# Adding products by a 1 MB transfer or on GpSimd in turns, and four more transposes on VectorE, in an embedding tower on one core

## What is computed

```python
e = jnp.stack([tbl_f[ids[:, f]] for f in range(40)], axis=1)     # 512 x 40 x 64, fp32
i_idx, j_idx = triu_indices(40, k=1)                             # 780 pairs
viW = einsum('bpd,pde->bpe', e[:, i_idx], W)                     # W: 780 x 64 x 64
z = einsum('bpe,bpe->bp', viW, e[:, j_idx])                      # 512 x 780
h = concatenate([z, dense_ctx], axis=1)                          # 512 x 796
h = maximum(h @ W_top1 + b_top1, 0)                              # 796 x 512
h = maximum(h @ W_top2 + b_top2, 0)                              # 512 x 256
y = h @ W_top3                                                   # 256 x 1
```

## Time and profile before

| what | us |
|---|---|
| median of three runs | 319.62 |
| span of the profiled execution | 361.1 |
| TensorE busy | 324.8 |
| VectorE busy | 255.2 |
| GpSimd busy | 206.5 |
| ScalarE busy | 106.8 |
| mean granted TensorE clock | 0.957 of full speed |

### The profile page before, as it was taken

How to read it: one execution, slowest core, us unless ns; L and a number is a source line. 1 busy time by engine, 2 the same in 40 slices (tenths; PEclk the granted TensorE clock), 3 DMA queues, 4 the chain that set the end, 5 groups by cost and what they waited for, 6 DMA issues and landing times.

```text
span 361.1 us, 4423 instructions
## 1 busy us (share of the span) xinstructions
PE 324.8 (90%) x1700; PEld 115.7 (32%) x1700; DVE 255.2 (71%) x249; ACT 106.8 (30%) x266; POOL 206.5 (57%) x178
## 2 busy tenths in 40 slices
PE   7999739699888949949959999989999999999997
PEld 2444213133222313312312333333333333333455
DVE  5996535586676856945847899999999999990000
ACT  0216000060505551350767653025049000001032
POOL 3887737354735625634654538989987677770000
PEclk9999988899989969987998999999999999999999
DMA  7941212112212272302211346867798766650000
GB/s 170 337 154 51 60 32 66 43 47 73 57 42 53 78 257 92 79 21 52 73 51 42 81 86 147 176 145 158 151 193 172 170 136 118 117 109 9 15 0 0
DMA packets 17772, 35.34 MB, mean 98 GB/s; under 512 B 3924, under 2 KB 4952, under 8 KB 17624
## 3 DMA queue, kind: packets, MB, share of 16 engines
q0 software_dynamic: 7408, 16.26, 23.4%
q1 hardware_dynamic: 7848, 13.96, 12.9%
q10 hardware_dynamic: 2496, 4.84, 3.9%
HBM read 22.86 MB, written 0.00 MB: 63 GB/s over the span
## 4 chain that ended last, share of the span: by engine, by line
PE 59%; DVE 19%; issue 8%; POOL 6%; another core or an unknown queue 6%; DMA 1%; ACT 0%; DVEq 0%; POOLq 0%
PE y_ps L664 33%; PE z_ps L687 15%; DVE prod L558 14%; PE y_ps L697 4%; POOL prod L378 3%; POOL gathered L349 2%; DVE prod L484 2%; PE t_ps L697 2%; PE y_ps L743 1%; PE t_ps L571 1%; POOL prod L374 1%; DMA lane_rows_sb<-lane_rows 1%; DVE zT L494 1%; DVE x_quad L490 1%
## 5 line engine op out<-in xcount | busy, mean ns | idle before, releaser
L664 PE MATMUL y_ps<-x,w 64*128 64x512 f32 x780 | 190.0, 619 | 29.6 <-DVE prod L558 21.9
L349 POOL DMA_INDIRECT gathered<-in_tbl,ids_sb x128 | 131.2, 1025 | 94.6 <-DVE prod L558 55.9
L558 DVE TENSOR_TENSOR prod<-y_ps,x 128x1024 f32<-128x1024 f32 x89 | 103.8, 1216 | 54.8 <-PE y_ps L664 27.5
L664 PEld LDWEIGHTS y_ps<-x,w 64*128 64x128 f32 x780 | 70.6, 189 | 146.6 <-issue 104.0
L558 DVE TENSOR_TENSOR prod<-y_ps,x_quad 128x1024 f32<-128x1024 f32 x96 | 110.6, 1215 | 3.8 <-PE y_ps L664 1.9
L687 PE MATMUL z_ps<-prod,select 128*32 128x512 f32 x596 | 81.7, 652 | 1.2 <-POOL prod L378 1.2
L417 ACT COPY x<-x_fold 32x128 f32<-32x128 f32 x176 | 52.0, 295 | 84.2 <-DVE x_fold L527 70.6
L378 POOL TENSOR_TENSOR prod<-prod 128x1024 f32<-128x1024 f32 x23 | 55.3, 2406 | 0.8
L374 POOL DMA_DIRECT2D prod<-prod x23 | 21.6, 939 | 22.4 <-DVE prod L558 16.3
L687 PEld LDWEIGHTS z_ps<-prod,select 128*32 128x32 f32 x596 | 15.3, 114 | 59.4 <-issue 39.5
L440 ACT COPY x_mix<-x 64x512 f32<-64x512 f32 x40 | 24.7, 616 | 0.7
(11 more groups left out here) (47 smaller groups left out, 84.8 us busy)
## 6 DMA issues: line engine op xcount, KB each, us to landing
w<-w_rows SPq DMA_DIRECT2D x48, 256.0 KB
prod<-prod POOLq DMA_DIRECT2D x23, 512.0 KB, 4.6
gathered<-in_tbl,ids_sb POOLq DMA_INDIRECT x128
w<-w_rows ACTq DMA_DIRECT2D x1, 1792.0 KB
prod<-in_tbl ACTq DMA_DIRECT2D x6, 256.0 KB
prod<-hot_ids SPq DMA_DIRECT2D x4, 256.0 KB, 3.9
prod<-in_tbl ACTq DMA_DIRECT2D x4, 128.0 KB, 3.3
w<-w_rows ACTq DMA_DIRECT2D x1, 512.0 KB
```

What stands on the lines that cost most here:

```text
L349: nc.gpsimd.indirect_dma_start(gathered[:, slot, c, s * DIM:(s + 1) * DIM], None, tables[f][:, :], bass.IndirectOffsetOnAxis(ap=ids_sb[:, ...
L558: nc.vector.tensor_tensor(prod[:, d % PROD_SLOTS, :, :], y_ps[:, d % DUO_SLOTS, :, :], factor, ALU.mult).then_inc(prod_ready, 1)
L664: last = nc.tensor.matmul(y_ps[:, d % DUO_SLOTS, half, :], w[rows, r % W_SLOTS, d % ROUND, :], x[rows, units[half], :], start=True, stop=True)
```

## The change

Units 12 and 13 become quads too (`PAIRED` 14 to 12), so that quads start at round 17 instead of 23 or 24. In rounds of `ADDED_BY_DMA` one accumulating DMA adds both duos (1 MB), in rounds of `ADDED_BY_POOL` one GpSimd instruction does (128x2048). 27 rounds are added: 17, 19, 21 and 24 to 47. Sums go three rounds behind (`LAG`). `FOLDED` starts at unit 5, `INSIDE` is 7, and 24 gathers are free at the start. With these `transposed_at` is 6 for units 5 and 6, 9 for unit 7, and 17, 25, 33, 41 for units 8 to 11; then 52, 60, 68, 80, 88, 100, 120, 144.

```diff
-LAG = 2
+LAG = 3
-PAIRED = 14
+PAIRED = 12
-FOLDED = range(9, 20)
-INSIDE = 3
-GATHERED_FIRST = 16
-ROUND_GATHERS = [4] * 24
-LATE_GATHERS = [1, 1, 2, 1, 1, 3, 1, 2, 1, 2, 1]
-UNADDED = [29]
+FOLDED = range(5, 20)
+INSIDE = 7
+GATHERED_FIRST = 24
+ROUND_GATHERS = [4] * 17 + [3] * 7
+LATE_GATHERS = [2, 1, 2, 1, 2, 1, 2, 1, 1, 1, 1]
+ADDED_BY_DMA = [17, 19, 21, 24, 26, 28, 30, 32, 34, 36, 38, 40, 42, 44, 46]
+ADDED_BY_POOL = [25, 27, 29, 31, 33, 35, 37, 39, 41, 43, 45, 47]
...
             for r in range(len(plan.rounds)):
-                if r in plan.added:
-                    done = gather_up_to(ROUND * r + ROUND - 1)
-                    nth = plan.added.index(r)
-                    low = ROUND * r % PROD_SLOTS
-                    pool.wait_ge(prod_ready, ROUND * r + 3)
+                done = gather_up_to(ROUND * r + ROUND)
+                low = ROUND * r % PROD_SLOTS
+                lows, highs = prod[:, low:low + 2, :, :], prod[:, low + 2:low + 4, :, :]
+                if r in ADDED_BY_DMA:
+                    nth = ADDED_BY_DMA.index(r)
+                    pool.wait_ge(prod_ready, ROUND * r + 4)
                     if nth >= PROD_ROUNDS:
                         pool.wait_ge(accumulated[nth % PROD_ROUNDS], 16 * (nth // PROD_ROUNDS))
-                    nc.gpsimd.dma_start(prod[:, low, :, :], prod[:, low + 2, :, :],
-                                        accum_op=ALU.add).then_inc(accumulated[nth % PROD_ROUNDS], 16)
-                    done = gather_up_to(ROUND * r + ROUND)
+                    nc.gpsimd.dma_start(lows, highs, accum_op=ALU.add).then_inc(accumulated[nth % PROD_ROUNDS], 16)
+                elif r in ADDED_BY_POOL:
                     pool.wait_ge(prod_ready, ROUND * r + 4)
-                    nc.gpsimd.tensor_tensor(prod[:, low + 1, :, :], prod[:, low + 1, :, :], prod[:, low + 3, :, :],
-                                            ALU.add).then_inc(added, 1)
-                else:
-                    done = gather_up_to(ROUND * r + ROUND)
+                    nc.gpsimd.tensor_tensor(lows, lows, highs, ALU.add).then_inc(added, 1)
...
-                if r in plan.added:
-                    nth = plan.added.index(r)
-                    pe.wait_ge(added, nth + 1)
+                duos = range(ROUND * r, ROUND * r + 2)
+                if r in ADDED_BY_DMA:
+                    nth = ADDED_BY_DMA.index(r)
                     pe.wait_ge(accumulated[nth % PROD_ROUNDS], 16 * (nth // PROD_ROUNDS + 1))
-                    duos = range(ROUND * r, ROUND * r + 2)
+                elif r in ADDED_BY_POOL:
+                    pe.wait_ge(added, ADDED_BY_POOL.index(r) + 1)
...
-            sum_round(len(plan.rounds) - LAG)
+            for r in range(len(plan.rounds) - LAG, len(plan.rounds) - 1):
+                sum_round(r)
```

More of the change, by code:

```diff
@@ L107, in __init__ @@
         self.gather_times()
-        self.added = [r for r in range(self.quad_start[0], len(self.rounds)) if self.is_quad(r) and r not in UNADDED]
+        assert all(self.is_quad(r) for r in ADDED_BY_DMA + ADDED_BY_POOL)
     def gather_times(self):
@@ L118, in gather_times @@
             after += [max(ROUND * r - 1, 1)] * count
-        assert len(ROUND_GATHERS) == self.quad_start[0] + 1 and len(after) == parts * (UNITS - HOT_UNITS)
+        assert len(after) == parts * (UNITS - HOT_UNITS)
         self.gather_after = after
```

## The result

The changed kernel takes 339.95 us (median of four runs, 339.28 to 340.61); the kernel before took 319.56 us beside it. The ratio is 1.0641, with a 95% interval of 1.0619 to 1.0662: slower by 20 us. Forecast were 337.0 us and a range of 326 to 343.

The account below looks back on a forecast made before the run. TensorE's own order was taken as the bound nearly throughout, VectorE close behind in added rounds. On 319.6 us, -3.4 - 1.2 - 2.4 + 0.6 + 16.6 + 4.3 + 2.9 = +17.4 gave 337.0 us, range 326 to 343.

Parts of the forecast that it names:

- The start: VectorE's queue waits for gathers of units 6 and 7 at their early transposes, and TensorE runs dry: +16.6 us.
- ScalarE's order at block 0: Unit 11's copies and mixtures stand ahead of block 0's copy in round 10, so sum 8 waits: +4.3 us.
- The duos stay 195: Regrouping leaves the count of duos at 195; only added rounds change, from 23 to 27.
- Four transposes off TensorE (-2.4): Units 5 to 8 leave TensorE, 4 x 0.59 us, for VectorE transposes and 16 ScalarE copies each: -2.4 us.
- Additions (-1.2): TensorE's present wait on GpSimd's addition goes: -1.2 us.
- Four more added rounds (-3.4): Added rounds go from 23 to 27, each saving TensorE 0.85 us in its sum: -3.4 us.
- Unit 18's transpose in an added round (+0.6): Unit 18 (duo 120, round 30) now meets an added round, where VectorE lacks time for its transpose: +0.6 us.
- neither wait is there, 313.2: Rival: gathers land before product 6 and ScalarE reaches its copy in time, 313.2 us; chance 0.05.
- The clock: TensorE's clock halves after the new waits, 1.7 us after sum 8 and 1.2 at the start: +2.9 us.
- Quicker gathers in the runs: Rival: gathers start 0.94 us apart in the runs, not 1.25; 332.4 us, or some 329; chance 0.05.
- ScalarE's wait alone, 319.2: Rival: the start is not exposed and only ScalarE's wait stays, 319.2 us; chance 0.05.
- The late transfer: Rival: the 1 MB transfer lands after its 12.0 us window; one us more costs 12, 349 us; chance 0.07.

Follow-up runs that it names:

- the second profile of before: The kernel before, unchanged, profiled once more: span 319.3 us in an execution of 321.1 us.
- the two mended kernels: Changed kernel with transposes of units 5 to 13 re-placed and two mixture-buffer sets, 321.06 us; same but units 5 to 8 transposed by TensorE, 320.84 us.
- the 16 gathers: Against the mended kernel with TensorE's transposes, only the first field of units 10 to 13 gathered, 16 gathers fewer: 315.85 us, ratio 0.9878.

## Why the prediction was right, and where it was not

**The start: right.** Foreseen were unit 6's landing at 45.8 (44.3), unit 7's at 55.8 (54.2), and the end of sum 1 at 69.4 (69.0). Against the second profile of before, whose TensorE stood there at 53.6, the start costs 15.4. That has the half clock in it, so it stands against 16.6 + 1.2 = 17.8: 2.4 less than foreseen. Of this 0.8 is the point of before (53.6, not 52.8), and some 1.5 is that the 24th gather started at 41.81, not 43.27. It varies between executions, from 41.81 to 45.46 in the profiles, so that part is luck. The landing was taken as 2.5 between bounds of 1.0 and 3.8 and is 2.5. The text's choice of starts 1.25 apart rather than spans of 0.94 was right too: by the spans the forecast would have been 332.4.

**ScalarE's order at block 0: right, the size a little small.** Foreseen were 4.3 of wait and 1.7 of half clock; the profile has 5.0 and 1.75. The rest of the 7.2 us between the sums is 0.4: unit 11's transpose itself waited 0.8 for its gathers. The runs without it gained 4.1; in the profile the difference lies in the start of that execution, and how it spreads over the runs stays open.

**Round 23: missed.** The step that failed is the regrouping, costed by the count of duos alone ("The duos stay 195"). A duo that was moved also moves the release of the buffer that it reads. It costs 4.2 us in the profile (sum 21 comes 8.80 after sum 20 instead of 4.63), 3.1 in the runs. The forecast's error of 3.0 is what is left of larger ones: 4.2 here and 1.2 at block 0 too little, 2.4 at the start too much. The mechanisms at the start and at block 0 are as foreseen; that 337.0 came within 1% is in part because these errors cancel.

**The terms of TensorE's work: true in the changed kernel, worth less once the waits are gone.** TensorE is busy 311.4 us, against 310.5 in the second profile of before. Of that 6.7 is half clock: four stretches of 3.1 to 3.5 us at 0.50, busy throughout. Without it TensorE's work is 5.8 less, which is 2.4 + 3.4. In the time, too, the terms add up: 15.4 + 7.2 + 4.2 - 3.4 - 1.2 - 2.4 + 0.6 = 20.4, as measured. They are not worth that by themselves. Four transposes off TensorE (-2.4): nothing, as the two mended kernels show, 321.06 and 320.84; ScalarE's 16 copies a unit come in between. Additions (-1.2): 0.3 to 0.6. Four more added rounds (-3.4): the regrouping that brings them needs unit 13 in round 17 instead of 20, and the new order asks for units 12 to 14 eight duos sooner; GpSimd's pace takes the gain back. Only with the transposes placed by that pace is 1.4 us left of all terms. Unit 18's transpose in an added round (+0.6) costs 0.4. The step that failed is the one behind the rival "neither wait is there, 313.2": it held that TensorE is the bound nearly throughout once the two waits are gone. It is not, over the first 14 units. The first profile hid it: from 36 to 162 us it has 71 gathers where the second has 97. Gathers are released by products, which came late there, so GpSimd's pauses looked like slack.

**The clock: right in kind.** 2.9 were foreseen. The profile has half-clock stretches after each of the four waits, as in the earlier trace rows; those after block 0 and round 23 cost about 1.7 us each (3.60 for 1.85 in the one seen above), and the latter was not foreseen. Those of the start partly fall into VectorE's pace, and no run parts the two. "Rounds of 4.63 from 27 on" came out, but for 5.00 twice, at the transposes of units 18 and 19, and no sum waits for a transfer for more than 0.8 us.

**The rivals.** Quicker gathers in the runs: no; from the 13th on the starts are 1.25 apart in every kernel's profile wherever nothing holds them back, and the profiled execution took 339.51 us, like the others. ScalarE's wait alone, 319.2: no, since the start is exposed. The late transfer: no, with 12.0 us of window and 7.9 of landing; a window of 7.4 makes it true.

## What to carry to other kernels

An instruction that waits costs its engine's whole queue, so its place is to be set by when its data lands: here eight gathers at 1.25 us, 10 us a unit, against the duo at which the transpose stands. When work is regrouped, list for each moved piece what it releases (a buffer, a semaphore, a bank), not only what it needs. And before gains on the busiest engine are added up, ask which engine would be the bound without them; the cheap test is to leave out some of that other engine's work, as with the 16 gathers, and see whether the time follows.

## What the runs showed of the hardware

- Two profiled executions of one program had spans of 361.1 and 319.3 us, mean granted clock 0.957 and 1.000. The second agrees with the runs to 1.7 us, the first does not.
- The first twelve gathers, issued while VectorE does its one-hot work, take up to 5.14 us each where later ones take 0.94, and which ones do differs between executions; the start of the 24th moves by up to 3.7 us, from 41.81 to 45.46. That VectorE's work is the reason is not shown.
- A 1 MB accumulating transfer inside SBUF lands 7.6 to 8.0 us after its issue (medians by kernel) where one of 512 KB took 4.6. In turns with GpSimd additions, and with a window of 12.0 us, they hide. Of three issued in consecutive rounds the second and third landed after 11.4 and 12.9 us and were waited for, 0.8 and 1.3 us.
- GpSimd adds 128x2048 in 4.57 us and 128x1024 in 2.41.
- A gather lands 2.5 to 2.7 us after its start (medians by kernel), and gathers issued without a pause start 1.25 us apart.
